# Two attention stages: query and key as two fp32r halves on quarters of the TensorE array instead of three bf16 parts on its halves, and row maxima transposed unsplit

## The chip, the core and the metric

The kernel runs on one core of one Trainium2 chip. The metric is the device time of one launch in microseconds. A profile of one execution says when each instruction ran; PE is TensorE (PEld its weight loads), DVE is VectorE, ACT is ScalarE, POOL is GpSimd and SP is SyncE, which here only issues DMAs.

## The reference

```python
x = x + attn_a(layernorm(x))      # [16, 512, 128], 16 heads of 8, causal, three heads re-weighted by position
x = x + ffn(layernorm(x))         # gated 128 -> 512 -> 512 -> 512 -> 128
x = x + attn_b(layernorm(x))      # 16 heads of 8, rotary position embedding, not causal
x = x + ffn(layernorm(x))         # the same weights again

scores = einsum('bhqd,bhkd->bhqk', q, k) / sqrt(8)
attn   = softmax(scores)          # max over k, exp, divide by the sum
out    = einsum('bhqk,bhkd->bhqd', attn, v) @ Wo + bo
```

## The kernel before

**Stages.** There are 16 sequences of 512 tokens, and x stays in SBUF throughout. The first attention ("causal") takes all sequences, then the feed-forward layer, then the second attention ("rotary"), then the feed-forward layer again. `program` gives each engine its own instruction stream; semaphores tie them together.

**One attention step.** An attention runs as a software pipeline with one sequence per step `n`. In step `n` the engines work on q, the transposed x and the norm of sequence n+1, on k and v of n, on the row maxima of n-1, on scores, exp and the weighting of v for n-2, on denominators of n-3 and on the output product of n-4. A step is cut into beats (20 causal, 32 rotary). A beat has one score job S (`scores`: two matmuls of up to 512 columns, one per head of a pair, into two of three ACT banks), one maximum job M (`maxes`: two matmuls into one of two DVE bank pairs), one weighting job W (`weigh`: four fp32 matmuls on four column quarters, each recorded as two) and now and then another product X (`misc_work`). `CAUSAL_AT` and `ROTARY_AT` say at which beat each job stands on each engine; "order" is the order on PE within a beat (MSWX causal, SMWX rotary). `Plan` writes out which head pair and which key or query tiles a beat takes.

**Exact scores in bf16.** q and k are split in three bf16 parts each, high, middle and low (`high`, `middle_low` on POOL, lines 663 to 680). Their six largest products are six terms of 8 rows, so a head's contraction has 48 rows. The rows are brought into place over DRAM: `store` (L580) writes the parts of one of q and k with six DMAs, `load` (L592) reads them back with two into `stack_q` and `stack_k`, head 0 of each pair on partitions 0 to 47, head 1 on 64 to 111. A score matmul has two more rows: the negated row maximum (as two bf16 parts) times ones, so that ACT's exp (L989) reads scores less their maximum.

**The maxima's way.** M (L1021; in the causal stage four small matmuls at L1038 add the mask to the diagonal tile) fills two banks; DVE reduces them to `negmax` (L868, L872); POOL splits half a sequence's maxima in two (`negated_max_parts`, L651, L653); PE transposes them (`turn_maxima`, L1072); ACT copies them (`nm_row`, L926); `aug` (L548) brings them into `stack_q` with two DMAs; the first score beat of a half waits for it (L996). In the causal stage POOL also sets the upper triangle of each exp tile to zero (L708), and W waits for that.

**SP's order.** SP issues all DMAs of a step in one fixed order (`sync`, lines 603 to 626): load q(n), aug of half 1 (n-2), the numerators of n-3 (L555, L558), store k(n), the reciprocals of n-3 (L563, which wait for DVE's L880 of beat 12 or 15), load k(n), spread the reciprocals (L570), aug of half 0 (n-1), store q(n+1).

```python
606  if n == 0: store(sp, n, "stored_k", 1)
607  if on(n, 0): load(sp, n, "stack_q", "stored_q", 0)
611  if on(n, 2): aug(sp, 1, n - 2)
613  if on(n, 3): numerators(sp, n - 3)
615  if n > 0 and on(n, 0): store(sp, n, "stored_k", 1)
617  if on(n, 3): store_reciprocals(sp, n - 3)
619  if on(n, 0): load(sp, n, "stack_k", "stored_k", 1)
621  if on(n, 3): spread_reciprocals(sp, n - 3)
623  if on(n, 1): aug(sp, 0, n - 1)
625  if on(n, -1): store(sp, n + 1, "stored_q", 0)
```

Each line stands for a condition and its call, written here on one line. The feed-forward stages multiply fp32r operands with all 128 rows (L1451) and are not changed but at their edges.

## Time and profile before

| | |
|---|---|
| median of 3 runs | 2139.06 us (2135.49 to 2146.88) |
| the profiled execution, its own time | 2145.3 us |
| its span | 2143.6 us |
| mean granted TensorE clock | 0.96 of 2.4 GHz |
| busy share of the span | PE 91%, DVE 80%, ACT 69%, POOL 51%, PEld 46% |
| chain that ended last, by engine | PE 48%, POOL 12%, SP's queue 10%, DMA 10%, issue 9%, DVE 7%, ACT 4% |

Times in the trace are microseconds from the span's start. A matmul's recorded length holds its way through the array, so two that follow each other overlap in the records: the distance from one start to the next is what a job costs PE. "PE busy" is counted from these lengths and reads high. "PEclk" is the granted clock as a share of 2.4 GHz; it has two levels, 1.0 and 0.5. In a wait row, `A <- B` is the idle time of A just before an instruction that B released. In the chain, each row is released by the one above it.

### The profile page before, as it was taken

The page shows a single profiled execution, that of the slowest core. Times are in us where ns is not written, and L with a number is a line of the kernel's source. Part 1 is how long each engine was busy: PE and PEld are TensorE (multiplying, and loading weights), DVE is VectorE, ACT ScalarE, POOL GpSimd, SP SyncE. Part 2 cuts the span into 40 slices and gives each one's busy share as a digit, 9 for nine tenths or more (in the row PEclk, how much of TensorE's full clock was granted, in tenths as well). Part 3 has the DMA queues.
Part 4 walks back from the last instruction along what each step waited for, and adds up shares of the span by engine and source line. Part 5 has one row for each costly group of instructions (what it writes and reads, how often), then busy time and mean ns, then how long its engine had stood idle before and what let it go on. Part 6 is the DMA issues. An engine that isn't in the chain of part 4 may idle for free.

```text
span 2143.6 us, 43057 instructions
## 1 busy us (share of the span) xinstructions
PE 1941.3 (91%) x16196; PEld 980.7 (46%) x16196; DVE 1719.6 (80%) x2342; ACT 1481.3 (69%) x2641; POOL 1097.3 (51%) x1553
## 2 busy tenths in 40 slices
PE   3789998899879999997899999999999978999998
PEld 1333333334337777774222222222222226777776
DVE  4888887788738888875889999899998936888883
ACT  1477777677766666652588888888887875666665
POOL 5777777677445555564423333434333014555554
PEclk9799999899989999998799999999999999999999
DMA  7456665656210000004344443344444100000000
GB/s 176 95 117 127 118 128 108 111 110 124 49 24 29 1 1 1 1 7 82 61 82 92 92 87 72 72 91 88 92 87 87 33 13 12 15 11 15 11 15 16
DMA packets 106357, 136.71 MB, mean 64 GB/s; under 512 B 21153, under 2 KB 90018, under 8 KB 100002
## 3 DMA queue, kind: packets, MB, share of 16 engines
q1 hardware_dynamic: 106146, 133.89, 31.2%
q8 instruction: 133, 2.18, 0.5%
q14 instruction: 78, 0.64, 0.1%
...
## 4 chain that ended last, share of the span: by engine, by line
PE 48%; POOL 12%; SPq 10%; DMA 10%; issue 9%; DVE 7%; ACT 4%; POOLq 0%; ACTq 0%; DVEq 0%
PE ps_score L1451 20%; PE ps_out L1061 7%; PE ps_max L1451 5%; PE ps_score L1003 5%; SPq L580 4%; DMA o_num<-o_raw 4%; DVE negmax L872 4%; PE ps_max L1021 3%; DMA d_stack<-parts 3%; PE ps_out L1451 3%; ACT prob L989 2%; DMA stack_q<-nm_rows 2%; POOL xhat L322 2%; PE ps_max L1102 2%; SPq L558 2%
## 5 line engine op out<-in xcount | busy, mean ns | idle before, releaser
L989 ACT ACTIVATE prob<-ps_score 128x512 f32<-128x512 f32 x1664 | 899.1, 597 | 209.1 <-PE ps_score L1003 191.0
L872 DVE TENSOR_REDUCE negmax<-ps_max 128x2 f32<-128x1024 f32 (+1 forms) x896 | 907.4, 1064 | 141.0 <-PE ps_max L1038 84.7
L1061 PE MATMUL ps_out<-prob,v_aug 128*9 128x256 f32 (+2 forms) x6656 | 518.9, 392 | 27.4 <-ACT o_raw L952 24.0
L1451 PE MATMUL ps_score<-h,w_hi 128*128 128x512 f32 x2048 | 503.5, 399 | 9.4 <-POOL h L1225 8.3
L1451 PEld LDWEIGHTS ps_score<-h,w_hi 128*128 128x128 f32 x2048 | 383.6, 189 | 104.3 <-POOL h L1225 10.8
L1003 PE MATMUL ps_score<-stack_q,stack_k 50*128 50x512 bf16 (+3 forms) x2048 | 360.3, 353 | 58.0 <-ACT prob L989 38.8
L1021 PE MATMUL ps_max<-stack_k,stack_q 48*128 48x512 bf16 (+3 forms) x2048 | 344.7, 355 | 56.4 <-DVE negmax L872 32.6
L708 POOL TENSOR_SCALAR_AFFINE_SELECT prob<-prob 128x256 f32<-128x256 f32 (+1 forms) x448 | 188.1, 440 | 154.9 <-ACT prob L989 154.6
L1213 POOL TENSOR_TENSOR h<-h3f,h 128x512 fp32r<-128x512 f32 x128 | 192.0, 1508 | 134.0 <-ACT h L1363 134.0
L1003 PEld LDWEIGHTS ps_score<-stack_q,stack_k 50*128 50x128 bf16 x2048 | 105.4, 94 | 313.9 <-ACT prob L989 237.0
L1061 PEld LDWEIGHTS ps_out<-prob,v_aug 128*9 128x9 f32 x6656 | 106.2, 89 | 305.9 <-ACT prob L989 148.6
L1213 POOL TENSOR_TENSOR h<-h2f,h 128x512 fp32r<-128x512 f32 x128 | 172.6, 1350 | 66.7 <-ACT h L1363 66.7
L1021 PEld LDWEIGHTS ps_max<-stack_k,stack_q 48*128 48x128 bf16 x2048 | 87.7, 95 | 217.6 <-DVE negmax L872 103.6
L668 POOL TENSOR_TENSOR qf<-qf,turned 128x512 f32<-128x512 f32 x31 | 39.7, 1280 | 261.6 <-DVE turned L849 261.6
L1357 ACT ACTIVATE h3f<-ps_score,s_col 128x512 f32<-128x512 f32 x128 | 87.5, 684 | 112.3 <-PE ps_score L1451 108.2
L1357 ACT ACTIVATE h2f<-ps_score,s_col 128x512 f32<-128x512 f32 x128 | 88.1, 688 | 95.2 <-PE ps_score L1451 89.1
L1267 DVE CAST h<-h1f 128x512 fp32r<-128x512 f32 x120 | 124.8, 1040 | 35.0 <-PE ps_score L1451 33.9
L1451 PE MATMUL ps_max<-ffn_xT,w_hi 128*128 128x512 f32 x512 | 144.7, 415 | 3.2 <-DVE ffn_xT L1274 2.5
L332 DVE TENSOR_SCALAR xhat<-x,mv,rstd 128x128 f32<-128x128 f32 x128 | 95.1, 803 | 44.1 <-POOL rstd L304 44.1
L1254 DVE SCALAR_TENSOR_TENSOR ut<-tanh,ps_max 128x512 f32<-128x512 f32 x128 | 86.8, 678 | 54.2 <-ACT tanh L1374 51.6
L1269 DVE TENSOR_TENSOR h<-h1f,h 128x512 fp32r<-128x512 f32 x120 | 115.3, 961 | 4.1
L1102 PE MATMUL ps_max<-xT,weights 128*128 128x512 f32 x176 | 107.4, 694 | 4.0 <-ACT xT L933 3.0
...
## 6 DMA issues: line engine op xcount, KB each, us to landing
d_stack<-parts SPq DMA_DIRECT2D x128, 192.0 KB, 2.8
...
d_stack<-parts SPq DMA_DIRECT2D x128, 128.0 KB, 2.8
d_stack<-parts SPq DMA_DIRECT2D x128, 64.0 KB, 2.4
o_num<-o_raw SPq DMA_DIRECT2D x128, 64.0 KB
o_rden<-d_rden SPq DMA_DIRECT2D x128, 64.0 KB
...
```

What stands on the lines that cost most here:

```text
L708: last = pool.affine_select(out=tri, in_=tri, compare_op=ALU.is_ge, fill=0.0, base=0, pattern=[[0, tri.shape[1]], [1, P]], channel_multipl ...
L872: last = dve.tensor_reduce(m["negmax"][:, t, :, p], banks[:, :, at:at + w], AX.X, ALU.max, negate=True)
L989: act.activation(prob(b, i)[:, o], act_bank("score", 2 * i + o), ACT.Exp).then_inc(s["prob"], 1)
L1003: mm = pe.matmul(act_bank("score", 2 * i + o)[:, at:at + w], m["stack_k"][c][rows, p, P * j:P * (j + 1)], m["stack_q"][c][rows, p, S - w:S ...
L1021: last = pe.matmul(to[:, o, at:at + w], m["stack_q"][c][rows, p, P * t:P * (t + 1)], m["stack_k"][c][rows, p, 0:w], start=(piece == 0), st ...
L1061: last = pe.matmul(m["ps_out"][32 * g:32 * g + HD + 1, out:out + w], m["v_aug"][b % VALUES][:, j, 4 * G + g, :], prob(b, beat)[:, g % 2, l ...
L1102: pe.matmul(to, m["weights"][:, which], m["xT"][:], start=True, stop=True).then_inc(s[f"{name}_ps"], 1)
L1213: pool.tensor_tensor(h[k][:, 1, f], hf[k][:, f % 2], h[k][:, 0, f], ALU.subtract).then_inc(s[f"h{k}"], 1)
L1267: dve.tensor_copy(h[1][:, 0, f], h1f[:, f % 2]).then_inc(s["h1_hi"], 1)
L1269: dve.tensor_tensor(h[1][:, 1, f], h1f[:, f % 2], h[1][:, 0, f], ALU.subtract).then_inc(s["h1"], 1)
L1357: act.activation(hf[k][:, f % 2], m["ps_hid"][:, f % 2], ACT.Gelu, scale=m["s_col"][:, k, f:f + 1]).then_inc(s[f"h{k}f"], 1)
L1451: mm = pe.matmul(to, w[:, cols], moving(part), start=begin and i == 0, stop=last and i == len(pairs) - 1)
```

## The change

q and k are split in two fp32r halves instead of three bf16 parts, in one go (`halves`: copy, subtract) at the beat where `high` stood, on whichever engine calls it. Three products of halves make three terms, 24 rows per head, so a head fits on a quarter (32 partitions) of the array and a matmul's operands are fp32r. Pair p takes the quarters 2(p%2) and 2(p%2)+1. The maximum job of a beat takes the other pair of a group than the score job does ("half in (1, 0)"), thus the other two quarters; the causal plan is rewritten over two groups at a time so that this holds there too, and the causal order on PE becomes SMWX. `store` has two DMAs instead of six and `load` four instead of two; the bytes are the same (768 KB each way for q and for k), in pieces of 2 KB instead of 1 KB on the store side. Maxima are transposed as fp32, without POOL's split; `aug` is one DMA with one row per head. The sizes: `stack_q` and `stack_k` hold 4 groups x 512 fp32r where they held 8 pairs x 512 bf16. The weights' flag (L804, L806 and its two DMAs) moves from the middle of the causal stage to its end.

```diff
-TERMS = 6
+TERMS = 3
 KROWS = TERMS * HD
-AUG = 2
+QUAD = P // 4
 SIDE = P // 2
 MASKED = -1.0e30
...
-    m["stack_k"] = [sb(f"stack_k{c}", [P, PAIRS, S], BF16) for c in range(STACKS)]
+    m["stack_k"] = [sb(f"stack_k{c}", [P, GROUPS, S], F32R) for c in range(STACKS)]
...
-    m["rest"] = sb("rest", [P, S])
-    m["parts"] = sb("parts", [P, 2, 3, S], BF16)
-    m["negmax"] = sb("negmax", [P, T, 2, PAIRS])
-    m["nm_parts"] = sb("nm_parts", [P, T, 2, 2, 2, HALF], BF16)
-    m["nm_rows"] = sb("nm_rows", [2 * 2 * HALF, 2, S], BF16)
+    m["parts"] = sb("parts", [P, 2, 2, S], F32R)
+    m["negmax"] = sb("negmax", [P, T, 2, 4, GROUPS // 2])
+    m["nm_rows"] = sb("nm_rows", [QUAD + H // 2, S], F32R)
...
-    m["d_stack"] = dram("d_stack", (2, 2, 2, TERMS, HD, PAIRS, S), BF16)
+    m["d_stack"] = dram("d_stack", (2, 2, TERMS, 4, HD, GROUPS, S), F32)
...
-CAUSAL_AT = {"k": 3, "nm1": 1, "v": 5, "proj": 8, "xT": 9, "nm0": 13, "q": 13, "weigh": (4, 5, 6, 7, 7), "out": 8,
-             "P_nm1": 0, "P_norm": 7, "P_v": 4, "P_bias": 11, "P_q1": 16, "P_q2": 17, "P_k1": 4, "P_k2": 8,
-             "P_nm0": 10, "P_o": 1, "D_stats": 6, "D_clear": 9, "D_q": 14, "D_k": 4, "A_v": 6, "D_bias": 6, "D_inv": 12,
-             "D_proj": 9, "A_nm1": 2, "A_nm0": 14, "A_xT": 10, "order": "MSWX"}
+CAUSAL_AT = {"k": 3, "nm1": 1, "v": 5, "proj": 8, "xT": 9, "nm0": 13, "q": 13, "P_norm": 7, "P_v": 4, "P_bias": 11, "P_q1": 16, "P_k1": 4,
+             "P_o": 1, "D_stats": 6, "D_clear": 9, "D_q": 14, "D_k": 4, "A_v": 6, "D_bias": 6, "D_inv": 12,
+             "D_proj": 9, "A_nm1": 2, "A_nm0": 14, "A_xT": 10, "order": "SMWX"}
...
+            for G in range(0, GROUPS, 2):
+                at = len(self.scores)
+                a, b = 2 * G, 2 * G + 2
+                for pair in (a, b):
+                    self.scores += [[(pair + half, 0, 0, S)] for half in range(2)]
+                    self.scores += [[(pair + half, 1, 0, 3 * P), (pair + half, 3, 3 * P, P)] for half in range(2)]
+                    self.diagonals += [(0,), (0,), (0, 3), (0, 3)]
+                    self.maxes += [[(pair + half, 0, 0, P), (pair + half, 2, P, 3 * P)] for half in (1, 0)]
+                    self.maxes += [[(pair + half, 3, 0, S)] for half in (1, 0)]
+                    if pair == a:
+                        self.scores += [[(a + half, 2, 0, 2 * P), (b + half, 2, 2 * P, 2 * P)] for half in range(2)]
+                        self.diagonals += [(0, 2)] * 2
+                        self.maxes += [[(a + half, 1, 0, 2 * P), (b + half, 1, 2 * P, 2 * P)] for half in (1, 0)]
+                blocks += [(at + 4, G, 1, 0, 0, S // 2, (0, 1), 0, True),
+                           (at + 5, G, 1, 0, S // 2, S // 2, (0, 1), S // 2, False),
+                           (at + 6, G, 3, 1, P, 3 * P, (2, 3), 0, False),
+                           (at + 7, G, 3, 3, 3 * P, P, (2, 3), 3 * P, False),
+                           (at + 8, G, 5, 2, 2 * P, 2 * P, (4, 5), 0, False),
+                           (at + 10, G + 1, 5, 2, 2 * P, 2 * P, (4, 5), 2 * P, True),
+                           (at + 10, G + 1, 7, 0, 0, S // 2, (6, 7), 0, False),
+                           (at + 11, G + 1, 7, 0, S // 2, S // 2, (6, 7), S // 2, False),
+                           (at + 12, G + 1, 9, 1, P, 3 * P, (8, 9), 0, False),
+                           (at + 12, G + 1, 9, 3, 3 * P, P, (8, 9), 3 * P, False)]
+                blocks[-10:] = [(when, g, at + read, j, out, w, tuple(at + x for x in where), lo, start)
+                                for when, g, read, j, out, w, where, lo, start in blocks[-10:]]
+                self.out_at += [at + 9, at + 13]
...
+                self.scores += [[(2 * G + half, j, 0, S)] for j in range(T) for half in range(2)]
+                self.diagonals += [()] * (2 * T)
+                self.maxes += [[(2 * G + half, t, 0, S)] for t in range(T) for half in (1, 0)]
...
         sp.wait_ge(s[f"nm_row{h}"], b + 1)
-        for o in range(2):
-            at = SIDE * o + KROWS
-            sp.dma_start(m["stack_q"][b % STACKS][at:at + AUG, HALF * h:HALF * (h + 1), :],
-                         m["nm_rows"][2 * HALF * o:2 * HALF * (o + 1), h, :]).then_inc(s[f"aug{h}"], 16)
+        sp.dma_start(m["stack_q"][b % STACKS][KROWS::QUAD, GROUPS // 2 * h:GROUPS // 2 * (h + 1), :].bitcast(F32),
+                     m["nm_rows"][QUAD * h:QUAD * h + H // 2].bitcast(F32)).then_inc(s[f"aug{h}"], 16)
...
         sp.wait_ge(s["parts"], count(2, b, i + 1))
-        for o in range(2):
-            parts = m["parts"][64 * o:64 * (o + 1), i]
-            rows = m["d_stack"][b % 2, i, o].rearrange("t d p n -> (d p) t n")
-            for part, (lo, hi) in enumerate(((0, 3), (3, 5), (5, 6))):
-                held = parts[:, part:part + 1].broadcast_to([64, hi - lo, S]) if i == 0 else parts[:, 0:hi - lo]
-                sp.dma_start(rows[:, lo:hi], held).then_inc(s[name], 16)
+        rows = m["d_stack"][b % 2, i].rearrange("t o d g n -> (o d g) t n")
+        parts = m["parts"][:, i].bitcast(F32)
+        if i == 0:
+            sp.dma_start(rows[:, 0:2], parts[:, 0:1].broadcast_to([P, 2, S])).then_inc(s[name], 16)
+            sp.dma_start(rows[:, 2:3], parts[:, 1:2]).then_inc(s[name], 16)
+        else:
+            sp.dma_start(rows[:, 0:2], parts).then_inc(s[name], 16)
+            sp.dma_start(rows[:, 2:3], parts[:, 0:1]).then_inc(s[name], 16)
...
-        sp.wait_ge(s[stored], count(96, b, 96))
-        for o in range(2):
-            rows = slice(SIDE * o, SIDE * o + KROWS)
-            sp.dma_start(m[name][b % STACKS][rows], m["d_stack"][b % 2, i, o].rearrange("t d p n -> (t d) p n"))\
-                .then_inc(s[name], 16)
+        sp.wait_ge(s[stored], count(32, b, 32))
+        for o in range(4):
+            rows = slice(QUAD * o, QUAD * o + KROWS)
+            sp.dma_start(m[name][b % STACKS][rows].bitcast(F32), m["d_stack"][b % 2, i, :, o]).then_inc(s[f"{name}{b % 2}"], 16)
...
+        if causal and n == B:
+            sp.wait_ge(f["halved"], 3)
+            sp.dma_start(m["d_flags"].rearrange("(p o) -> p o", o=1), m["flags"][:]).then_inc(f["flag_moved"], 16)
...
-    def negated_max_parts(pool, b, h):
-
-        pool.wait_ge(s["max"], count(MAXES, b, MAXES // 2 * (h + 1)))
-        wait(pool, s[f"nm_ps{h}"], b)
-        full = m["negmax"][:, :, :, HALF * h:HALF * (h + 1)]
-        parts = m["nm_parts"][:, :, h]
-        pool.tensor_copy(parts[:, :, :, 0], full).then_inc(s["nmh"], 1)
-        pool.wait_ge(s["nmh"], count(2, b, h + 1))
-        pool.tensor_tensor(parts[:, :, :, 1], full, parts[:, :, :, 0], ALU.subtract).then_inc(s["nm"], 1)
...
+    def halves(eng, b, name, i):
...
+            eng.wait_ge(s[f"{name}_turn"], b + 1)
+            eng.wait_ge(s[f"{name}_main"], b + 1)
+            eng.tensor_tensor(m["qf"][:, i], m["qf"][:, i], m["turned"][:, i], ALU.add).then_inc(s[name], 1)
+        eng.wait_ge(s[name], b + 1)
+        wait(eng, s["stored_q" if i == 0 else "stored_k"], count(32, b))
+        wait(eng, s["highs"], count(2, b, i))
+        eng.tensor_copy(m["parts"][:, i, 0], m["qf"][:, i]).then_inc(s["highs"], 1)
+        eng.wait_ge(s["highs"], count(2, b, i + 1))
+        wait(eng, s["parts"], count(2, b, i))
+        eng.tensor_tensor(m["parts"][:, i, 1], m["qf"][:, i], m["parts"][:, i, 0], ALU.subtract).then_inc(s["parts"], 1)
...
+            to = m["negmax"][:, t, p // HALF, 2 * (p % 2):2 * (p % 2) + 2]
+            last = dve.tensor_reduce(to, banks.rearrange("p o (c k) -> p o c k", k=w), AX.X, ALU.max, negate=True)
...
         act.wait_ge(s[f"nm_ps{h}"], b + 1)
-        wait(act, s[f"aug{h}"], count(32, b))
-        act.activation(m["nm_rows"][:, h, :], act_bank(f"nm{h}")[0:16, 0:S // 2].bitcast(BF16), ACT.Copy)\
+        wait(act, s[f"aug{h}"], count(16, b))
+        act.activation(m["nm_rows"][QUAD * h:QUAD * h + H // 2], act_bank(f"nm{h}")[0:H // 2], ACT.Copy)\
             .then_inc(s[f"nm_row{h}"], 1)
...
-            pe.wait_ge(s[f"aug{h}"], count(32, b, 32))
+            pe.wait_ge(s[f"aug{h}"], count(16, b, 16))
         pieces = plan.scores[i]
         for piece, (p, j, at, w) in enumerate(pieces):
             for o in range(2):
-                rows = slice(SIDE * o, SIDE * o + KROWS + AUG)
+                at_row = QUAD * (2 * (p % 2) + o)
+                rows = slice(at_row, at_row + KROWS + 1)
                 if piece == 0:
                     act_bank_free(pe, n, "score", 2 * i + o)
                 mm = pe.matmul(act_bank("score", 2 * i + o)[:, at:at + w],
-                               m["stack_k"][c][rows, p, P * j:P * (j + 1)], m["stack_q"][c][rows, p, S - w:S],
+                               m["stack_k"][c][rows, p // 2, P * j:P * (j + 1)], m["stack_q"][c][rows, p // 2, S - w:S],
                                start=(piece == 0), stop=True, skip_group_check=(piece > 0))
                 if piece == len(pieces) - 1:
                     mm.then_inc(s["score"], 1)
...
-                rows = slice(SIDE * o, SIDE * o + KROWS)
-                last = pe.matmul(to[:, o, at:at + w], m["stack_q"][c][rows, p, P * t:P * (t + 1)],
-                                 m["stack_k"][c][rows, p, 0:w], start=(piece == 0), stop=True,
+                at_row = QUAD * (2 * (p % 2) + o)
+                rows = slice(at_row, at_row + KROWS)
+                last = pe.matmul(to[:, o, at:at + w], m["stack_q"][c][rows, p // 2, P * t:P * (t + 1)],
+                                 m["stack_k"][c][rows, p // 2, 0:w], start=(piece == 0), stop=True,
                                  skip_group_check=(piece > 0))
...
-        pe.wait_ge(s["nm"], count(2, b, h + 1))
+        pe.wait_ge(s["max"], count(MAXES, b, MAXES // 2 * (h + 1)))
         act_bank_free(pe, n, f"nm{h}")
         for t in range(T):
-            last = pe.transpose(act_bank(f"nm{h}")[0:16, P // 2 * t:P // 2 * (t + 1)].bitcast(BF16),
-                                m["nm_parts"][:, t, h].rearrange("p a b c -> p (a b c)"), m["ident_b"][:])
+            last = pe.transpose(act_bank(f"nm{h}")[0:H // 2, P * t:P * (t + 1)],
+                                m["negmax"][:, t, h].rearrange("p a b -> p (a b)"), m["ident"][:])
         last.then_inc(s[f"nm_ps{h}"], 1)
...
+        if l == 0:
+            left["flag_of_weights"](dve)
...
-    return np.array([(2 * p + o) * HD + d for o in range(2) for d in range(HD) for p in range(PAIRS)])
```

## Rows read from the trace of the kernel before

**Rows 1.** Windows: length; busy of PE, PEld, DVE, ACT, POOL; PEclk, DMA share, GB/s.

```profile
99.00:583.00 484.00, 431.33 (x5666) 185.30 (x5666) 397.81 (x558) 359.06 (x680) 341.28 (x694) 0.95 0.58 112
...
975.00:1121.00 146.00, 121.65 (x855) 41.23 (x853) 115.06 (x127) 79.75 (x145) 60.46 (x86) 0.84 0.34 66
1121.00:1667.00 546.00, 515.17 (x4986) 146.47 (x4985) 496.03 (x541) 455.71 (x855) 192.06 (x280) 1.00 0.44 87
```

**Rows 2.** Chain that ended last, in time order, one causal step (start, length, work).

```profile
251.34 1.16 POOL rest L673
...
260.55 1.17 POOL parts L680
261.74 0.63 SPq L580
...
265.05 2.46 DMA d_stack<-parts
...
271.25 0.69 SPq L548
271.98 4.42 DMA stack_q<-nm_rows
276.45 0.61 PE ps_score L1003
```

**Rows 3.** Timeline, DVE, same step (start, length, engine, line, work).

```profile
262.77 0.54 DVE L880 RECIPROCAL rden<-den 128x64 f32<-128x64 f32 x1
```

**Rows 4.** Windows, the first 3.5 us after that step's boundary.

```profile
242.20:245.70 3.50, 3.47 (x26) 0.83 (x27) 1.75 (x2) 1.81 (x4) 1.88 (x4) 0.51 0.84 179
```

**Rows 5.** Timeline, PE, one causal beat and the next one's start.

```profile
249.51 0.39 PE L1021 MATMUL ps_max<-stack_k,stack_q 48*128 48x512 bf16 x2
249.73 0.22 PE L1038 MATMUL ps_max<-ident_s,mask_q 64*128 64x64 bf16 x4
249.79 0.38 PE L1003 MATMUL ps_score<-stack_q,stack_k 50*128 50x256 bf16 x4
250.11 0.62 PE L1061 MATMUL ps_out<-prob,v_aug 128*9 128x256 f32 x8
250.66 0.39 PE L1021 MATMUL ps_max<-stack_k,stack_q 48*128 48x128 bf16 x4
```

**Rows 6.** Timeline, PE, one rotary beat and the next one's start.

```profile
1402.10 0.39 PE L1003 MATMUL ps_score<-stack_q,stack_k 50*128 50x512 bf16 x2
1402.33 0.38 PE L1021 MATMUL ps_max<-stack_k,stack_q 48*128 48x512 bf16 x2
1402.64 0.62 PE L1061 MATMUL ps_out<-prob,v_aug 128*9 128x256 f32 x8
1403.19 0.43 PE L1003 MATMUL ps_score<-stack_q,stack_k 50*128 50x512 bf16 x2
```

**Rows 7.** Groups of instructions by form (busy us, mean ns of one | idle before).

```profile
L1451 PE MATMUL ps_score<-h,w_hi 128*128 128x512 f32 x2048 | 503.5, 399 | 9.4 <-POOL h L1225 8.3 <-ACT h2f L1357 0.8 <-ACT h3f L1357 0.3
...
L1451 PEld LDWEIGHTS ps_score<-h,w_hi 128*128 128x128 f32 x2048 | 383.6, 189 | 104.3 <-POOL h L1225 10.8 <-issue 1.7 <-ACT h2f L1357 1.2
...
L1213 POOL TENSOR_TENSOR h<-h2f,h 128x512 fp32r<-128x512 f32 x128 | 172.6, 1350 | 66.7 <-ACT h L1363 66.7
...
L1003 PEld LDWEIGHTS ps_score<-stack_q,stack_k 50*128 50x128 bf16 x2048 | 105.4, 94 | 313.9 <-ACT prob L989 237.0 <-issue 48.6 <-DMA stack_q<-nm_rows 22.5
...
L671 POOL CAST parts<-qf 128x512 bf16<-128x512 f32 x63 | 38.7, 615 | 17.5 <-DVE qf L839 15.5
```

**Rows 8.** Timeline, POOL, key splits of one rotary step.

```profile
1374.12 1.16 POOL L673 TENSOR_TENSOR rest<-qf,parts 128x512 f32<-128x512 f32 x1
...
1391.46 1.16 POOL L680 TENSOR_TENSOR parts<-rest,parts 128x512 bf16<-128x512 f32 x1
```

**Rows 9.** Waits, causal stretch 99 to 583 us (total, times, longest).

```profile
DVE negmax L872 <- PE ps_max L1038: 65.6, 89, 8.8
```

**Rows 10.** Waits, rotary stretch 1121 to 1667 us.

```profile
DVE negmax L872 <- PE ps_max L1021: 32.2, 47, 2.1
```

168 lines of the change are left out of this document (44 added, 124 removed).

## The prediction

> **What bounds the kernel now.** I read the windows by stage first [rows 1], then the chain through one step of each attention, then PE's timeline beat by beat, then the waits of the engine that is busiest. The feed-forward stages are not touched, so everything must come from the two attentions and their edges.
>
> The causal stretch from 99 to 583 us holds 14 steps, 34.6 us each. DVE is busy 397.8 of its 484 us, 28.4 a step. The chain [rows 2] shows a loop that closes once a step: POOL subtracts the high part of k (251.34), does masks and a norm, ends the low part at 261.7, SP issues six stores, the last lands at 267.5, loads and the spread of reciprocals follow, the two DMAs of aug are issued from 271.25, and 4.42 us later, at 276.45, PE may start the first scores of the next step. PE had waited there, and at the same place one step earlier the granted clock was 0.51 over the next 3.5 us [rows 4]. Within a beat PE runs without gaps: 0.28 us for M and its mask, 0.32 for S, 0.55 for W [rows 5], 1.15 in all; beats with split pieces take more. So the causal stage alternates between PE and this loop. A second way into the same place is DVE's reciprocal at 262.77 [rows 3], which SP could send only behind the stores of k.
>
> The rotary stretch from 1121 to 1667 us holds 12 steps of 45.5 us. DVE is busy 496.0 of 546 us, 41.3 a step, ACT 38.0, at a full clock. A beat costs PE 0.23 for S, 0.31 for M and 0.55 for W, 1.09 [rows 6], 35 a step; with the projections, the output product and the transposes its recorded busy time is 515.2/12 = 42.9 of 45.5 [rows 1]. DVE and PE are both close to being the bound. DVE's idle time behind M is 32.2 us, 2.7 a step [rows 10]; in the causal stage it is 65.6, 4.7 a step [rows 9].
>
> **The change, part by part.**
>
> PE, S beside M. The two matmuls of a pair already run together on two halves of the array: S starts at 1402.10 and M, two matmuls of 512 columns later, at 1402.33, the time of one [rows 6]. With four quarters S and M can share that time. I take off the smaller of the two: 0.23 a beat, 32 x 0.23 = 7.4 us a rotary step, 20 x 0.23 = 4.6 a causal one. An fp32r operand costs about what bf16 does: 2048 feed-forward matmuls of 512 columns fill 503.5 us, 0.25 each against 0.23 [rows 7]. fp32r on quarters is not in this trace. The bounds are "as halves in bf16", which gives the figures above, and "one after the other", four times 0.25 instead of 0.54, which is the second rival. I take the first, since rows 6 show the same kind of sharing on the same array.
>
> The Trainium skill, "TensorE: Matmul & The Clock Gate", section "Measured speedup vs the span model", gives 3.07x for four 32-row tiles at 512 columns. By that estimate S and M together would take about 4 x 0.23 / 3.07 = 0.30 us, which would leave the same sum. No row here shows four at once.
>
> Weight loads. They grow from 94 to 189 ns [rows 7]. Four a beat, in pairs, lie beside W's 0.55 us unless PE waits for a bank; then each such wait is up to 0.1 us longer. That makes at most 32 x 0.1 = 3.2 us of PE a rotary step, and I take half.
>
> Switching between array shapes. S before M follows in 0.23, S before W in 0.32 [rows 5, 6], so a switch costs about 0.09. In the causal stage the mask's four matmuls now stand between quarters and columns, one switch more a beat: 20 x 0.09 = 1.8 us of PE. PE per causal step: 431.3/14 = 30.8 recorded [rows 1], less 4.6, less some 1.7 for the slow stretch (below), plus 1.8 and some loads, near 27. DVE's 28.4 covers that; without this cover it would show in full. The Trainium skill, "TensorEngine Tiling (Array Packing)", section "Key Properties", states that changing the tiling mode drains the engine. By that rule a switch would cost up to the 0.39 - 0.21 = 0.18 us that a recorded matmul is longer than its columns, 3.6 a causal step, PE would be at 29, level with DVE, and about 1 us a step of the gain would go.
>
> POOL. One copy and one subtraction replace two of each. The copy was 0.62 [rows 7]; to fp32r it lies between that and the 1.35 of an fp32r subtraction [rows 7]. Two passes of 1.0 and 1.3 against 3.5 us: 1.2 less for each of q and k, and 0.46 less for each of two maxima splits. POOL is no bound. What counts is when k is ready: the subtraction at 251.34 [rows 2] is then the last one, so k is done near 253 instead of 261.7, and in the rotary stage at about 1375.5 instead of 1392.6 [rows 8].
>
> SP and DMA. Stores 6 to 2, loads 2 to 4, aug 2 to 1, counted a store at 0.63, an aug at 0.69 [rows 2], and a load, which has no row here, at a store's 0.63: for one of q or k 2.5 less and 1.3 more. Bytes are the same; the store pieces are twice as large, so I expect no slower landing. Nothing waits longer behind a load: what is queued behind it is the numerators, which come up to 1.9 us sooner, aug's second DMA included. What is late next in the causal stage is the reciprocal: it stays at beat 12 of DVE, and from its end (263.3) come 0.6 for the store, about 2 for landing, 2.8 for four spreads, 0.7 for aug and 4.4 for landing, 10.5 us. PE has eight beats till then, about 12 us. So the loop opens by some 1.5 us, and the stall and the slow clock behind it (3.5 x 0.5 = 1.7 us) go in most steps.
>
> **The sum.** Causal: of DVE's 34.6 - 28.4 = 6.2 idle us a step, 4.7 of them behind M's mask, I take 3.4 off, because over half of it stands at the step's boundary and in beats where PE is behind. That leaves 31.2 a step, DVE 91% busy, the share it already reaches in the rotary stage: 15 steps x 3.4 = 51. Rotary: of 2.7 us I take 1.6; the waits at projections, which share DVE's banks, stay: 15 x 1.6 = 24. Edges: at the start, at 975 to 1121 us (clock 0.84 [rows 1]) and at the second sequence of the rotary fill, the path parts, stores, landing, load is walked with nothing beside it. Each time 1.2 on POOL and 2.5 - 1.3 on SP go, 2.4 us: 7, and 3 for a fill that gets past its slow clock sooner, 10. The moved flag costs nothing: its DMAs land while DVE still works on the last maxima of the causal stage; uncovered they would be two landings, 4 us once. 51 + 24 + 10 = 85. The profiled execution took 2145.3 us, so 2060; the median stands 6 lower, which gives 2054, and I say 2055.
>
> **The rivals.**
>
> 1. The relief is not DVE's. PE gets faster, but M still waits for DVE's banks and the chain is replaced by POOL's masks and the reciprocal. Then only the slow-clock piece and part of the boundary goes: 1.7 x 15 in the causal stage, 0.3 x 15 in the rotary one, 8 at the edges, together 38, giving 2100. For it: the rotary steps have a full clock and DVE is at 91%. Against: the idle time behind M is there in both [rows 9, 10].
> 2. fp32r on quarters does not share the array. Then a rotary beat is 4 x 0.25 + 0.55 + 0.09 = 1.64 instead of 1.09; PE goes from 42.9 to 60.5 a step, 15 over 45.5: 15 x 15 = 225. Causal 20 x 0.49 = 9.8 on 30.8, 40.6 or 6 over 34.6: 90. Together 2139 + 315 = about 2450. It decides as soon as PE passes DVE's 41.3, which is at 0.87 for S and M together instead of about 0.3. Nothing in the trace speaks for it.
> 3. The clock falls. PE has less to do, so it idles more, and the clock was seen at its lower level after an idle stretch [rows 4] and in the thin part of the fill. PE would need 37 us a rotary step and 27 a causal one at full clock; DVE's bound is passed when the mean clock falls below 37/43 = 0.86 and 27/30 = 0.9. At 0.7 they need 53 and 38.6: 15 x 7.5 + 15 x 4 = 172, less 10 at the edges, giving 2300; at 0.8, 46 and 34, about 2130. This one ends slower below 0.8. Against: at 0.94 recorded PE busy share the rotary stretch had real gaps and a clock of 1.00 [rows 1].
>
> That the change does not do what it says (S and M issued, but never together, because M's bank is late) is within rival 1, at the same price, for then DVE is the bound.
>
> **How the numbers follow.** Forecast 70%; rival 1, 15%; rival 3 in its slower form 7%, near no change 3%; rival 2, 5%. About 0.5%, 10 us, is what a measurement of this kernel can tell from no change. Faster 0.85, same 0.03, slower 0.12. If all of DVE's waits but 1 us a step went, the steps would be 29.4 and 42.3: 78 + 48 + 12 less, 2001; I set the low end at 2010. The high end takes in rival 1 with some room: 2112.
>
> **What would show it.** In the changed profile M should start a few hundredths behind S, not 0.23, and a beat's W 0.3 behind S. A steady causal step near 31 us, a rotary one near 44, DVE at 91 and 94% there. The aug landing should end no wait at the boundary, and the granted clock in 99 to 583 us should rise from 0.95. k's parts should be ready by beat 6 of the causal step. I would be wrong if fp32r matmuls start one after another, if PE's clock in the rotary stage leaves 1.00, if masks on POOL hold W, or if SP now waits for the reciprocal until aug is late.

## The result, and the profile after

The changed kernel took 2345.19 us (median of 4 runs, 2337.74 to 2360.84) against 2139.96 us for the kernel before: a ratio of 1.0965, with a 95% interval of 1.0899 to 1.1032. The forecast was 2055 us, faster; its range ended at 2112. It was wrong in sign and by 290 us. Where single runs of a kernel took over 1.5% longer than its shortest, its ratio below leaves them out and its median does not.

The profile page of the changed kernel, its engine shares, the slices of clock and DMA, and the head of the chain that ended last:

```profile
PE 2101.7 (89%) x16196; PEld 1139.4 (48%) x16196; DVE 1722.8 (73%) x2340; ACT 1482.3 (63%) x2641; POOL 974.5 (41%) x1297
...
PEclk6679797988866999998699998988899875999999
DMA  4233232332211000001222212222222110000000
...
PE 59%; DMA 13%; POOL 7%; SPq 7%; issue 6%; ACT 4%; DVE 3%; POOLq 0%; ACTq 0%; DVEq 0%
```

Every engine is busy for a smaller share of the span than before, only the weight loads for a slightly larger one (48% for 46%), and DMA holds 13% of the chain (before 10%). So the kernel waits more. The windows of the two attentions of after, with the columns of [rows 1]:

```profile
99.00:583.00 484.00, 412.49 (x4764) 196.05 (x4762) 339.98 (x484) 305.50 (x574) 256.78 (x512) 0.84 0.30 98
...
1121.00:1667.00 546.00, 486.57 (x4192) 186.90 (x4194) 450.54 (x493) 378.84 (x716) 134.70 (x177) 0.88 0.22 75
```

DVE is busy for 340 us where it was 398, the clock is 0.84 and 0.88 where it was 0.95 and 1.00 [rows 1]. From one issue of the augmenting rows to the same one a step later, a causal step takes about 40 us (before 34.6), a rotary one 51 (before 45.5). The chain through the end of one causal step (start, length, work) answers to [rows 2]:

```profile
309.07 0.72 SPq L586
...
311.28 0.69 SPq L562
...
313.43 0.65 SPq L562
...
314.13 9.04 DMA stack_q<-nm_rows
323.17 0.04 issue
323.21 0.55 PE ps_score L953
```

The small transfer of the augmenting rows takes 9.04 us where one took 4.42 [rows 2]. In the waits of 99 to 583 us (total, times, longest) PE stands for it once a step, and DVE behind PE for twice as long as in [rows 9]:

```profile
DVE negmax L823 <- PE ps_max L989: 131.9, 103, 6.3
...
PE ps_score L953 <- DMA stack_q<-nm_rows: 61.8, 11, 6.1
```

Why that transfer is late is not in any row of time, but in the trace's semaphore events. A DMA's semaphore rises once when it is issued, or not at all, and then once for each DMA engine that has landed its part: for the four loads of a key in the changed kernel, four times soon after the issues and twelve times later, three a load. Counted over all key loads of each kernel (the last three kernels are experiments below), with the median time from a group's first issue to its last landing, and the same for the augmenting rows:

```
kernel          loads of one key   outer dims   engines a load   group landed   augmenting rows landed
before          2                  48 | 48      16               6.9 us         5.1 us
after           4                  24 | 3       3                13.2 us        8.8 us
a_load8         4                  24 | 8       8                7.7 us         3.3 us
a_load12        4                  24 | 24      12               6.7 us         2.8 us
b_load3         4                  24 | 3       3                13.0 us        8.8 us
```

The four key loads of after land at 5.7, 8.2, 10.6 and 13.2 us after the first issue (medians), in three parts each, one load behind the other as on the same three engines. The destination has 24 rows, but the source lies as 3 terms of 8 rows with other quarters between, so its outermost dimension is 3. The Trainium skill, "DMA: Bandwidth & Descriptors", section "Why a DMA increments its semaphore by 16 and not by 1", states that a DMA runs on the largest number of engines up to 16 that divides the slowest dimension of both patterns, on the lowest-numbered ones. By that rule 24 and 3 give 3, 24 and 8 give 8, 24 and 24 give 12; the traces agree in each case. The augmenting rows of after land in four parts. The first is there 1.8 us after the issue (median), at most 2.2; the other three come together after 8.6 to 8.8 us (medians). In a_load8 all four come together, after 3.1 to 3.3 us. That is what is to be expected if three of the four engines are those that still carry the loads, and the fourth is free.

### The profile page after: what moved, and what is told of

Its sections match the earlier page's. It is cut to its first block, busy times and chain, and to the rows that moved or that the text cites. A ratio compares the mean times of both kernels' runs of the same rounds, so it can differ in the third digit from the quotient of the medians.

```text
span 2359.1 us, 42607 instructions
## 1 busy us (share of the span) xinstructions
PE 2101.7 (89%) x16196; PEld 1139.4 (48%) x16196; DVE 1722.8 (73%) x2340; ACT 1482.3 (63%) x2641; POOL 974.5 (41%) x1297
## 4 chain that ended last, share of the span: by engine, by line
PE 59%; DMA 13%; POOL 7%; SPq 7%; issue 6%; ACT 4%; DVE 3%; POOLq 0%; ACTq 0%; DVEq 0%
PE ps_score L1400 18%; PE ps_out L1010 14%; PE ps_score L953 11%; DMA o_num<-o_raw 6%; DMA stack_q<-nm_rows 5%; PE ps_max L1400 5%; SPq L586 3%; PE ps_out L1400 2%; ACT prob L938 2%; PE ps_max L972 2%; POOL xhat L317 2%; SPq L562 2%; PE ps_max L1050 2%; SPq L550 2%; PE ps_max L1080 1%
## 5 line engine op out<-in xcount | busy, mean ns | idle before, releaser
L823 DVE TENSOR_REDUCE negmax<-ps_max 128x2 f32<-128x1024 f32 (+2 forms) x896 | 912.1, 1064 | 306.6 <-PE ps_max L989 190.2
L1010 PE MATMUL ps_out<-prob,v_aug 128*9 128x256 f32 (+2 forms) x6656 | 582.0, 434 | 54.7 <-ACT o_raw L901 52.5
L953 PE MATMUL ps_score<-stack_q,stack_k 25*128 25x512 f32 (+3 forms) x2048 | 525.7, 481 | 98.4 <-DMA stack_q<-nm_rows 77.6
L972 PE MATMUL ps_max<-stack_k,stack_q 24*128 24x512 f32 (+3 forms) x2048 | 468.6, 490 | 48.5 <-DVE negmax L823 19.7
L953 PEld LDWEIGHTS ps_score<-stack_q,stack_k 25*128 25x128 f32 x2048 | 242.3, 203 | 510.6 <-ACT prob L938 221.6
L972 PEld LDWEIGHTS ps_max<-stack_k,stack_q 24*128 24x128 f32 x2048 | 197.1, 207 | 76.6 <-issue 37.6
L901 ACT ACTIVATE o_raw<-ps_out 128x512 f32<-128x512 f32 x128 | 76.7, 599 | 59.1 <-DMA o_num<-o_raw 43.4
```

Of the source, the lines that this page charges most:

```text
L823: last = dve.tensor_reduce(m["negmax"][:, t, p // HALF, side:side + 2, p // 2 % 2], banks[:, :, at:at + w], AX.X, ALU.max, negate=True)
L953: mm = pe.matmul(act_bank("score", 2 * i + o)[:, at:at + w], m["stack_k"][c][rows, p // 2, P * j:P * (j + 1)], m["stack_q"][c][rows, p // ...
L972: last = pe.matmul(to[:, o, at:at + w], m["stack_q"][c][rows, p // 2, P * t:P * (t + 1)], m["stack_k"][c][rows, p // 2, 0:w], start=(piece ...
L1010: last = pe.matmul(m["ps_out"][32 * g:32 * g + HD + 1, out:out + w], m["v_aug"][b % VALUES][:, j, 4 * G + g, :], prob(b, beats[g // 2])[:, ...
```

## The experiments

### The loads

**a_load8**: the rows of a quarter in the order (d, t) instead of (t, d), for q and k alike, so that the outermost dimension is 8.

```diff
-            sp.dma_start(m[name][b % STACKS][rows].bitcast(F32), m["d_stack"][b % 2, i, :, o])
+            sp.dma_start(m[name][b % STACKS][rows].bitcast(F32), m["d_stack"][b % 2, i, :, o].rearrange("t d g n -> d t g n"))
...
```

> The changed kernel with one edit: the rows of each quarter of the stacks are ordered (d, t) instead of (t, d), for q and k alike, so that the outermost dimension of each load is 8 instead of 3. Theory 1 (the loads ran on 3 DMA engines, one after the other, and the augmenting rows, numerators and stores stood behind them; the stalls, and the slow clock after each, are the loss): a load's pieces land on 8 engines, the fourth of a group lands about 7 to 8 us after the first is issued instead of 13.4, the 9.0 us landing of the augmenting rows falls towards 5, the causal step falls from 40 to 33 to 35 us, the rotary one from 51 to 44 to 46, the granted clock in the two stretches returns above 0.93, and the time is 2050 to 2140. Theory 2 (fp32r on quarters draws the clock down or costs PE more by itself): the landings are short, but the clock stays at 0.84 and 0.90 and the time stays above 2250. Theory 3 (S and M together cost 0.42 instead of the expected 0.3 us, with a weight load of 181 ns exposed): the landings and the clock come back, but PE is the bound: rotary steps of 46 to 48 us and 2130 to 2200 in all.

Measured: 2177.81 us, ratio 1.0186 (1.013 to 1.0242). Landings as theory 1 said, and 167 us came back, but the time is above all of theory 1's range. Its windows, and two of its waits from 99 to 583 us:

```profile
99.00:583.00 484.00, 456.72 (x5452) 219.14 (x5450) 385.04 (x539) 348.25 (x654) 285.03 (x571) 0.89 0.39 109
1121.00:1667.00 546.00, 518.81 (x4936) 197.67 (x4928) 493.06 (x543) 445.04 (x848) 146.13 (x192) 0.97 0.26 81
```

```profile
PE ps_score L954 <- ACT prob L939: 20.2, 16, 1.4
...
PEld ps_score L954 <- DMA stack_q<-nm_rows: 5.9, 4, 1.5
```

The wait for the augmenting rows is nearly gone. Undisturbed steps are 33.8 and 45.3 us, no more than level with the 34.6 and 45.5 of before, and those with a slow clock 36 to 40 and 47 to 48.

**a_load12**: the DRAM stack with the quarter outermost, `(2, 2, 4, HD, TERMS, GROUPS, S)`, loads of 24 merged rows, three stores of one term each.

> The changed kernel with the DRAM stack laid out with the quarter outermost, so that a load's 24 rows are one dimension (24 and 24), and three stores of one term each instead of two. Theory 1: each load runs on 12 engines, lands about as fast as or a little faster than on 8, SP's third store costs 0.7 us a q or k, and the time is within 1% of the run with 8 engines. Theory 2: short landings, and the clock stays at 0.84 and 0.90, above 2250 us. If the engine count of a load is not given by the outer dimension at all, the landings of this run and of the one with 8 differ from that: 3 engines again would leave 2345.

Measured: 2184.19 us, 1.0203 (1.0169 to 1.0236): the same within 1%. From 8 engines on, faster loads bought nothing. SP's issuing is not what made the difference between after and a_load8 either: an issue of a load takes 0.68 us in the one and 0.65 in the other (0.36 here).

**b_load3**: the kernel before, with only its loads cut as in the changed one. The terms become an outer dimension of its DRAM stack, `(2, 2, TERMS, 2, HD, PAIRS, S)`, and each load's semaphore becomes two, used by turns.

```diff
-        for o in range(2):
-            rows = slice(SIDE * o, SIDE * o + KROWS)
-            sp.dma_start(m[name][b % STACKS][rows], m["d_stack"][b % 2, i, o].rearrange("t d p n -> (t d) p n"))
+        for o, u in ((0, 0), (0, 1), (1, 0), (1, 1)):
+            rows = slice(SIDE * o + 24 * u, SIDE * o + 24 * (u + 1))
+            sp.dma_start(m[name][b % STACKS][rows], m["d_stack"][b % 2, i, 3 * u:3 * (u + 1), o])
...
```

> The kernel before with its loads alone changed: four pieces of 24 rows of 8192 bytes with an outermost dimension of 3, instead of two of 48 rows; the same bytes, the same stores, bf16 on halves as before. Theory 1: the pieces run on 3 DMA engines and the last of a group lands near 13 us after the first issue instead of 6.6, the two DMAs of the augmenting rows are held up behind them (9 us instead of 4.4), the causal step grows from 34.6 to 38 to 41 us, the rotary from 45.5 to 48 to 51, the clock falls below 0.95, and the time is 2230 to 2330. Theories 2 and 3 (the loss lies in the matmuls): the landings are late but hidden, 2135 to 2165 us, clock 0.95 in the causal stretch and 1.00 in the rotary one.

Measured: 2377.43 us, 1.1115 (1.1083 to 1.1147), more than theory 1 gave it. The new matmuls are not in this kernel, and yet it shows the symptoms of after: causal steps of 41 us, rotary ones of 54, the clock at 0.86 and 0.88, and the late landing in its chain:

```profile
99.00:583.00 484.00, 388.05 (x4693) 161.91 (x4689) 332.69 (x478) 298.98 (x564) 296.95 (x596) 0.86 0.36 96
1121.00:1667.00 546.00, 450.46 (x3928) 122.72 (x3928) 424.41 (x463) 358.10 (x670) 169.35 (x248) 0.88 0.26 71
```

```profile
329.38 8.12 DMA stack_q<-nm_rows
```

Its PE works on maxima before scores in the causal stage, so there it waits for the loads themselves. The first load of a key is issued at 322.77 us, the last part of the fourth lands at 335.71, and the first maximum job (PE's timeline) starts right behind it:

```profile
335.80 0.59 PE L1020 MATMUL ps_max<-stack_k,stack_q 48*128 48x128 bf16 x4 [4.13 <-issue]
```

Such waits sum to 40.0 us in 99 to 583 us (11 times), those for the augmenting rows to 8.7; in the rotary stretch the latter are 68.3.

So the cut of the loads alone makes either kernel slower, by 167 and 238 us. In b_load3 SP's share is in the 238: four issues of 0.70 us instead of two of 0.4. What is left open is the 38 us by which a_load8 is slower than before, and the 123 by which it misses the forecast.

### Sharing the array

**a_load8_same**: a_load8 with the maxima of a beat on the quarters of its scores (`for half in (1, 0)` in the plan of the causal maxima and of the rotary ones made `for half in range(2)`).

> The changed kernel with the rows ordered (d, t) as in the run with 8 engines, and with the maxima of a beat on the same quarters as its scores (the reversal of the two pairs is undone), so that S and M can no longer run at the same time. If the sharing of the array is worth what the trace suggests, a full beat's S and M take 0.50 to 0.60 instead of 0.42 us, 32 x 0.1 = 3 to 5 us a rotary step of PE time, and the time is 40 to 120 us above the run with 8 engines. If DVE is the bound there, or the sharing gives nothing, the two are within 15 us. Theory 2 would let it come out faster, as PE is busier and its clock higher.

Measured: 2436.81 us, 1.1159 (1.107 to 1.1247). Its four runs lie between 2372 and 2496 us and the profile is of the longest; by the ratio it is some 210 us above a_load8, where 40 to 120 were expected. One full-clock rotary beat of a_load8 (PE's timeline), then of this kernel:

```profile
1450.09 0.50 PE L954 MATMUL ps_score<-stack_q,stack_k 25*128 25x512 f32 x2
1450.10 0.50 PE L973 MATMUL ps_max<-stack_k,stack_q 24*128 24x512 f32 x2
1450.53 0.62 PE L1011 MATMUL ps_out<-prob,v_aug 128*9 128x256 f32 x8
1451.08 0.75 PE L954 MATMUL ps_score<-stack_q,stack_k 25*128 25x512 f32 x2
1451.34 0.49 PE L973 MATMUL ps_max<-stack_k,stack_q 24*128 24x512 f32 x2
1451.76 0.62 PE L1011 MATMUL ps_out<-prob,v_aug 128*9 128x256 f32 x8
1452.31 0.51 PE L954 MATMUL ps_score<-stack_q,stack_k 25*128 25x512 f32 x2
```

```profile
1450.54 0.53 PE L954 MATMUL ps_score<-stack_q,stack_k 25*128 25x512 f32 x2
1450.88 0.43 PE L973 MATMUL ps_max<-stack_k,stack_q 24*128 24x512 f32 x2
1451.23 0.62 PE L1011 MATMUL ps_out<-prob,v_aug 128*9 128x256 f32 x8
```

With sharing, S and M start 0.01 apart where no bank is waited for, and W follows after 0.42 to 0.44; without, after 0.69. Four quarters do run at once. The rotary step grows by the 3 us expected, 48.4 against 45.3. The causal one does not fit: mostly 54 to 61 us, in stretches of up to 222 us at the lower clock. The two shortest runs had mean clocks of 0.866 and 0.880 where a_load8's profile has 0.927, so the lower clock is theirs too.

### What paces a beat

The beats of a_load8 above are 0.99 and 1.23 long by turns, 1.11 on average, no better than the 1.09 of [rows 6]. In the second one the other score matmul waits 0.25 us for its bank. ACT's timeline beside it:

```profile
1450.68 3.31 ACT L939 ACTIVATE prob<-ps_score 128x512 f32<-128x512 f32 x6 [0.16 <-PE ps_score L954]
1453.87 0.60 ACT L902 ACTIVATE o_raw<-ps_out 128x512 f32<-128x512 f32 x1
```

Six exponentials end to end in 3.31 us, 0.55 each, two a beat: 1.10. Two runs leave out a quarter of that work.

**a_load8_exp384**, **b_exp384**: after the first sequence, the exponentials cover columns 128 to 511 only.

```diff
-                act.activation(prob(b, i)[:, o], act_bank("score", 2 * i + o), ACT.Exp)
+                act.activation(prob(b, i)[:, o, P * (b > 0):], act_bank("score", 2 * i + o)[:, P * (b > 0):], ACT.Exp)
```

> The changed kernel with loads on 8 engines, and each exponential of the scores (after the first sequence of each attention) over the last 384 of 512 columns: a quarter of ACT's exponentials is left out, nothing else changes. Two exponentials of one pair start 0.494 us apart for 512 columns, about 0.96 ns a column, so a beat's two should cost ACT 0.25 us less. Theory 4 (a plain beat is paced by ACT's two exponentials over three score banks, 1.11 us, so the 0.12 us that S beside M saves PE buys nothing): plain rotary beats fall from 1.11 to about 0.97 (PE's own 0.42 + 0.55), a rotary step from 45.4 towards DVE's 41 to 43, the waits of scores for exponentials go, fewer slow clocks, and the time falls from 2178 to 2060 to 2110. Rival (PE or DVE paces the beats, or the clock does): the time falls by less than 20 us.

> The kernel before with the same quarter of its exponentials left out. There a beat costs PE 1.09 us and ACT 1.09 us. By theory 4 PE stands right behind ACT in it, so the plain beats stay at 1.09 and the time falls by only 0 to 30 us from 2139; and the changed kernel with loads on 8 engines, freed of ACT in the same way, would then be the faster of the two. If the time falls by as much as the changed kernel's, ACT paces both and the new array use buys nothing in either.

Measured: 2119.81 us, 0.9917 (0.9891 to 0.9943), and 2128.56 us, 0.9963 (0.9944 to 0.9982). The changed kernel gains 58 us, which leaves it 10 above the expected 2060 to 2110; the one before gains 10. Undisturbed steps of a_load8 go from 33.8 to 31.4 and from 45.3 to 44.1, and its time at the lower clock from 320 to 258 us, so not all of the 58 is ACT's own. ACT holds the new array use back more than the old: before, two exponentials (1.10) and PE's beat (1.09) stood level. It is a part of the gap, not the whole, and not a limit by itself: with bf16 operands (below) the steps come to 30.8 and 43.7 us with every exponential in place.

### The order of a beat, and the clock

**a_load8_causal_ms**, **a_load8_ms**: `"order": "SMWX"` made `"MSWX"` in the causal plan, and in both.

> The changed kernel with loads on 8 engines, and the causal order of a beat put back to maxima before scores (MSWX). If the new order is what makes PE stand 1.37 us in front of the scores with the maxima behind it, DVE gets its maxima earlier, the causal step of 33.8 (clean) and 36 to 38 (with a slow clock of 10 us) goes to 33 to 34, and the time is 2120 to 2160. If ACT paces the causal beats, the wait only moves and the time stays within 15 us of 2178.

> As the last one, with the rotary order put to maxima before scores as well. In the rotary stage the second score matmul waits 0.25 us for its bank in every second beat with the maxima behind it. If that wait holds DVE up, the rotary step falls from 45.4 to 44 to 45 us, 5 to 20 us below the run with only the causal order changed. If it is ACT's pace, the rotary step stays; if the sharing is lost when the maxima start first (0.25 and then the scores alone), it grows by up to 4 us a step, 60 in all.

Measured: 2488.29 us, 1.1637 (1.1611 to 1.1663), and 2500.09 us, 1.169 (1.1661 to 1.1718). No theory had this. The causal order makes nearly all of it; with the rotary order changed too, undisturbed rotary steps go from 45.3 to 45.7 us. The mask now stands between M and S, so that the two share nothing in the causal stage, and the clock stays down. A window of a_load8_ms (columns as in [rows 1]) and PE's timeline in it:

```profile
392.00:702.00 310.00, 308.59 (x1892) 135.74 (x1890) 136.25 (x195) 123.11 (x227) 103.98 (x207) 0.50 0.22 63
```

```profile
501.10 0.79 PE L973 MATMUL ps_max<-stack_k,stack_q 24*128 24x512 f32 x2
501.82 0.29 PE L990 MATMUL ps_max<-ident_s,mask_q 64*128 64x64 bf16 x4
502.04 0.79 PE L954 MATMUL ps_score<-stack_q,stack_k 25*128 25x384 f32 x4
```

PE is busy for 308.59 of 310 us, its S and M on quarters of the array, and the granted clock is 0.50, the 1.2 GHz level, the whole time. A causal step of 34 us becomes one of 65. Waiting is thus not the only thing that keeps this clock low. The Trainium skill, "TensorE: Matmul & The Clock Gate", section "What's actually happening", states that the throttled state is the default and that activity releases it. By that rule the throttle would be released in this window, in which PE is hardly ever idle. The trace does not agree, and the measurement decides.

### fp32r

**a_load8_bf16**, **a_load8_causal_ms_bf16**: score and maximum matmuls read only the upper 16 bits of each fp32r value, as bf16 with a stride of two, from the same tiles (the same edit in both). The low bits are left out.

```diff
-m["stack_k"][c][rows, p // 2, P * j:P * (j + 1)]
+m["stack_k"][c][:].bitcast(BF16)[rows, p // 2, 2 * P * j + 1:2 * P * (j + 1):2]
```

> The changed kernel with loads on 8 engines, and its score and maximum matmuls on the upper 16 bits of each fp32r value, read as bf16 with a stride of two from the same tiles: the low bits of every operand are left out, rows, columns, quarters and order stay. Theory 5a (fp32r is what costs: 181 ns weight loads, a matmul of 0.50 instead of 0.39 us, S and M 0.42 instead of 0.31): a plain S and M takes about 0.31, recorded matmuls are 0.39 long, second scores wait less, steps of 32 to 33 and 44 to 45 us, a time of 2100 to 2150. Theory 5b (the small number of rows in use, a quarter of the array a matmul, is what the clock and the length come from): within 20 us of 2178, with S and M at 0.42.

> The run with the causal order maxima before scores, which stood at the lower clock for 310 us on end with PE 99% busy, with the same bf16 reading of the operands. If fp32r is what keeps the clock down, it leaves the low level and the time falls below 2250; if it is quarters of the array one pair after the other, with a mask between, it stays between 2400 and 2500.

Measured: 2077.02 us, 0.9708 (0.9667 to 0.9749), below theory 5a's range, and 2249.75 us, 1.054 (1.0497 to 1.0583), right at the bound of its first case. With the data type alone 101 us go, and the kernel is faster than the one before. The groups by form, a_load8 and then a_load8_bf16 (busy us, mean ns of one | idle before):

```profile
L954 PE MATMUL ps_score<-stack_q,stack_k 25*128 25x512 f32 x1280 | 390.0, 517 | 37.6 <-ACT prob L939 31.2 <-issue 6.4
...
L973 PEld LDWEIGHTS ps_max<-stack_k,stack_q 24*128 24x128 f32 x2048 | 188.3, 197 | 59.6 <-DVE negmax L824 36.7 <-issue 18.4 <-DVE negmax L820 1.8
```

```profile
L954 PE MATMUL ps_score<-stack_q,stack_k 25*128 25x512 bf16 x1280 | 317.3, 411 | 41.5 <-ACT prob L939 29.3 <-issue 6.0 <-DMA stack_q<-nm_rows 5.3
...
L974 PEld LDWEIGHTS ps_max<-stack_k,stack_q 24*128 24x128 bf16 x2048 | 83.9, 93 | 75.4 <-DVE negmax L824 49.3 <-issue 17.3 <-DVE negmax L820 1.9
```

A weight load is 93 instead of 197 ns (means over both levels of the clock), a recorded matmul of 512 columns 411 instead of 517, and W follows S and M after 0.33 us instead of 0.43. Time at the lower clock, added up over the profiled execution, falls from 320 to 227 us (after: 603, before: 173). In the causal order MSWX it falls to 484 us, from 999 in the profile of the longest run (2537 us), or from some 830 to 870 by the mean clocks of the other four (an estimate).

**a_bf16_load3**: the same reading as bf16 in the changed kernel with its loads as they were.

> The changed kernel with its loads as they are (3 DMA engines), and its score and maximum matmuls on the upper 16 bits of each fp32r value, read as bf16: the low bits of every operand are left out. If the loads and fp32r are two causes that add, this run stands 168 us above the one with both mended (2077), at 2245. If the wait for the loads hides what fp32r costs, it stays above 2300; if the clock, which fp32r lowers, is what makes the loads hurt, it falls below 2180.

Measured: 2290.61 us, 1.0699 (1.0652 to 1.0746). The expectation had 2245 if the two causes add and over 2300 if one hides the other; it is between. bf16 is worth 101 us with 8 engines, 55 with 3; the loads cost 167 with fp32r and 214 with bf16. So the two do not add: with the slow loads in place, 46 us less come back for bf16.

### The wait at the slow clock

In a_load8 the clock falls about once a step, near places where PE waits. Three runs move PE work there or away.

**a_load8_proj18**, **a_load8_proj18_both**: causal `"proj": 8` to 18 and `"D_proj": 9` to 19; in the second also rotary 14 to 18 and 15 to 19. **a_load8_v8**: `"v"` from 5 to 8 and from 15 to 18, `"A_v"` one beat behind each.

> The changed kernel with loads on 8 engines, and in the causal attention the output projection moved from beat 8 to beat 18 (its DVE part from 9 to 19). In the trace of the run with 8 engines PE runs ahead over beat 19, which has no weighing, and then waits 1.37 us for an exponential; the clock falls there for 3.4 to 10 us, once a step. Theory 6 (PE's idle stretch at the step's boundary is what costs the clock): about 1 us of PE work put in front of it shortens the wait to 0.4 us or less, the slow clocks of the causal stretch fall from 102 to under 60 us, the step goes from 33.8 to 36 towards 32 to 33.5, and the time is 2130 to 2160. Rival (the clock falls for the small share of the array in use, with or without the wait): the slow clocks stay and the time is within 15 us of 2178.

> As the last one, with the rotary projection moved from beat 14 to 18 too, in front of the transposes of x, for which PE waits 0.5 us for POOL and loses the clock for 6.8 us in about every third step. Theory 6: those slow clocks (34 us in the rotary stretch) go, rotary steps stay at 45.3, 10 to 20 us less than the last run. Rival: no difference beyond 8 us.

> The changed kernel with loads on 8 engines, and the product for v moved from beat 5 to 8 in the causal attention and from 15 to 18 in the rotary one (ACT's copy of it one beat behind each): about 1 us of PE work in front of the beat with the transposes of x, where PE waits for POOL. Taking the output projection away from the same place cost 35 us. Theory 6 (PE's wait there starts the slow clock): the wait falls by up to 1 us, the slow clocks of the causal stretch fall from 102 to under 70 us, the causal step to 33 to 34.5, the time to 2130 to 2160. Rival (the projection's move hurt in another way, as by its DVE part at beat 19): within 15 us of 2178.

Measured: 2212.6 us (1.0348, 1.0313 to 1.0383), 2204.7 us (1.0322, 1.0285 to 1.0359) and 2190.14 us (1.0259, 1.0187 to 1.0332). The first was a misreading: the beat without weighing that precedes the transposes of x is number 9, and the projection at beat 8 had covered it. The waits between 110 and 580 us, of a_load8 and of a_load8_proj18:

```profile
PE ps_score L1037 <- POOL xhat L317: 6.0, 12, 0.7
```

```profile
PE ps_score L1037 <- POOL xhat L317: 18.4, 12, 1.5
```

The wait tripled, time at the lower clock in 99 to 583 us rose from 102 to 132 us, and the kernel lost 35. With the rotary projection moved too, the kernel took 8 us less than that, at the edge of what the rival allowed, and the rotary stretch had 15 us at the lower clock instead of 27. The move in the other direction did take the wait away and in the rotary stretch all of its 34 us at the lower clock; but rotary steps went from 45.3 to 45.8, the causal stretch had 120 us at the lower clock instead of 102, and the scores waited longer for exponentials. So theory 6 fits the rotary stretch and not the causal one, where the wait went and the slow clock stayed. Neither move gained time.

### A version that beats both

**quarters_bf16**: a_load8 with two true bf16 halves instead of fp32r ones. Tiles, DRAM stack and `nm_rows` are BF16 and the `bitcast(F32)` of the DMAs are gone, and the bytes are halved. It keeps two bf16 parts of each operand where the kernel before keeps three, so it is less exact than that. **quarters_bf16_v8** adds the move of v, **quarters_bf16_same** takes the sharing away, **quarters_bf16_again** repeats the first.

> [...] If PE's cost is what matters, as the reading as bf16 suggests, the time is 2060 to 2080, at most 15 us below 2077, since the loads already wait for nobody. If transfers of half the size relieve the start and the steps' boundary as well, it is 2040 to 2060.

> The last one with the product for v in front of the transposes of x, at beats 8 and 18. With theory 6 there is less to win here, as only 3.4 us of slow clock a step are left in bf16: 5 to 20 us below the last run. If the wait moves elsewhere, within 5 us.

> Quarters with true bf16 halves and loads on 8 engines, with the maxima of a beat on the same quarters as its scores, so that S and M cannot run together. If the sharing is worth PE's time alone, a beat's S and M take 0.54 instead of 0.33 us, as in the kernel before: 4 us a causal step, 1 to 3 a rotary one (ACT paces the plain beats there), 60 to 100 us in all, 2130 to 2170. If the stretches at the lower clock, which made the fp32r kernel without sharing 259 us slower, come with bf16 too: 2250 or more. If the gain lies in the smaller work and not in sharing: below 2100.

> The kernel with quarters and true bf16 halves once more, unchanged, for its ratio: 2060 to 2080, 0.96 to 0.975 of the kernel before.

Measured: 2072.0 us (0.9663, 0.9612 to 0.9715), 2084.53 (0.9739, 0.9698 to 0.9781), 2211.57 (1.0378, 1.0325 to 1.043; the medians alone give 1.033), and in the repeat 2071.12 (0.9675, 0.9655 to 0.9696). The windows of the repeat:

```profile
99.00:583.00 484.00, 439.55 (x5884) 173.83 (x5884) 401.68 (x588) 385.46 (x726) 306.07 (x617) 0.95 0.28 68
1121.00:1667.00 546.00, 506.86 (x5174) 165.04 (x5175) 499.15 (x552) 462.99 (x895) 130.35 (x171) 0.98 0.19 48
```

Halving the bytes gave 5 us over the reading as bf16, within the spread: little of its time was still a wait for transfers. The move of v, from which 5 to 20 us were expected, lost 12. Without sharing the kernel is 140 us slower, most of it in the causal stage (steps of 33 to 47 us instead of 30.7) and with spells of 41 us at the lower clock there in bf16 too. So without the sharing nothing of the gain over before is left, and part of what sharing gives is a clock that stays up.

## Why the prediction was wrong, step by step

- **SP and DMA, "Bytes are the same; the store pieces are twice as large, so I expect no slower landing."** This step failed, and gave the sign. The loads were counted by their issues on SP and by their bytes, not by the engines they run on; 16 became 3. "Nothing waits longer behind a load" fell with it: the augmenting rows landed after 8.8 us instead of 5.1. It measured 167 us, and 238 in the kernel before. The issues were mis-sized too: a load was taken at 0.63 us, two before and four after; two of 0.4 became four of 0.68, 1.9 us more for each of q and k instead of 1.3. a_load12, with issues of 0.36 and one store more, was no faster than a_load8, so no time is seen to hang on that.
- **"An fp32r operand costs about what bf16 does"**, from 0.25 against 0.23 a matmul in [rows 7]. Wrong for these matmuls: S and M together are followed after 0.43 us, not about 0.3, and with bf16 after 0.33. Together with its effect on the clock it measured 101 us with 8 engines. The feed-forward rows show fp32r back to back on the whole array; they could not show it on quarters between two switches of the array's shape. The margin was also thinner than the working says. It put the point from which PE passes DVE's 41.3 at 0.87 for S and M together, which comes out of plain beats (35 us) set against the whole step (45.5). With its own 37 for PE and 0.31 for S and M it is 0.31 + (41.3 - 37)/32 = 0.44, and fp32r's 0.43 stands right there.
- **S beside M.** Right: the four matmuls start 0.01 us apart, and rival 2 (no sharing) is excluded. In the causal stage the gain was smaller than the 0.23 a beat taken off, since the mask no longer hides behind anything: in a_load8 (PE's timeline below) S and M take 0.49 and the mask 0.22 before W, 0.71 in all, against 0.60 in [rows 5], where the pieces are somewhat different. The step named one switch more of 0.09, not the mask's own time.

```profile
388.70 0.50 PE L954 MATMUL ps_score<-stack_q,stack_k 25*128 25x512 f32 x2
388.71 0.55 PE L973 MATMUL ps_max<-stack_k,stack_q 24*128 24x128 f32 x4
389.19 0.29 PE L990 MATMUL ps_max<-ident_s,mask_q 64*128 64x128 bf16 x4
389.41 0.83 PE L1011 MATMUL ps_out<-prob,v_aug 128*9 128x384 f32 x8
```

- **The relief goes to DVE.** Right once fp32r and the loads are out of the way, which in the kernel as changed they are not. Freed of both, undisturbed steps are 30.8 and 43.7 us (31.4 and 44.5 on average) where 31.2 and 44 were forecast, and the wait of DVE in the causal stretch falls from 65.6 [rows 9] to 48.1. The working left out ACT, whose two exponentials of 0.55 us already filled the beat; it takes part in what a_load8 lost, but did not keep the bf16 kernel from these steps.
- **Rival 3, the clock.** It had 7% and was priced by PE idling more. The clock did fall, to 0.84 and 0.88 in the two stretches, and the time went the way that this rival named. But its price does not fit: it ends slower only below 0.8. The idling was that of the loads, and in other runs unshared work on quarters, in fp32r above all, kept the clock low without any.
- **Weight loads** went from 94 to between 194 and 207 ns on average, as taken. Whether four a beat lie beside W's 0.55 us, as the working has it, no run shows; how fp32r's 0.1 us splits between load and matmul was not measured by itself.
- **The sum.** With both causes out of the way (a_load8_bf16) the kernel takes 2077, 22 above the forecast; fp32r adds 101 and then the loads 167, which gives the 2345 measured. In the other order it is 214 for the loads and 55 for fp32r, so neither figure is the price of its cause by itself. How near it comes is partly luck: the forecast was for fp32r operands, and neither the mask's own time nor ACT was in it.

Open are why fp32r lowers the clock, what in the work on quarters keeps it low while PE is busy, and how much a three-part operand as exact as before would cost on quarters: it was not tried.
